# Query and key weights of a cross attention multiplied once at the start, the per-batch query product taken out, and part of a memory read issued as a transpose

## What is computed

```python
# end of the first block
out = Y * silu(gate) @ w_out.T
...
reads = jnp.moveaxis(reads, 0, 1).reshape(B, L, D)
out = out + ALPHA * (reads @ w_read.T)
return residual + out
...
# cross attention of Q (tokens) over K = V (context)
q = Q @ Wq + bq
k = K @ Wk + bk
v = V @ Wv + bv
scores = jnp.einsum('bqd,bkd->bqk', q, k) * scale
scores = jnp.where(pad_mask == 0, jnp.float32(-1000000000.0), scores)
w = jax.nn.softmax(scores, axis=-1)
out = jnp.einsum('bqk,bkd->bqd', w, v)
out = out @ Wo + bo
```

## Time and profile before

| what | value |
|---|---|
| median of three runs | 873.61 us |
| span of the profiled execution, first to last instruction | 869.8 us |
| PE busy | 830.7 us (96%) |
| ACT busy | 736.7 us (85%) |
| DVE busy | 725.3 us (83%) |
| POOL busy | 166.0 us (19%) |
| DMA, mean rate | 26 GB/s |

### The profile page before, as it was taken

One profiled execution on the slowest core, in us unless ns is written; L12 is line 12 of the kernel. 1 busy time (PEld: TensorE's weight loads), 2 busy tenths in 40 slices (PEclk: granted clock), 3 DMA queues, 4 the chain that ended last, 5 costly groups with the idle time before them and its releaser, 6 DMA issues.

```text
span 869.8 us, 21262 instructions
## 1 busy us (share of the span) xinstructions
PE 830.7 (96%) x7966; PEld 584.0 (67%) x7966; DVE 725.3 (83%) x2189; ACT 736.7 (85%) x1407; POOL 166.0 (19%) x198
## 2 busy tenths in 40 slices
PE   7899999999999999999999999999999999998874
PEld 4676767777767767777767767676767677654432
DVE  3653578989898999989898989999898988897775
ACT  3887789899898989899998989898998989784633
POOL 7101120312031131313120211312120310211110
PEclk9999999999999999999999999999999999998988
DMA  6100101010010101010100101001000000000000
GB/s 190 50 14 4 38 3 38 5 38 16 2 39 16 37 17 38 16 37 17 38 15 2 39 16 38 29 25 29 25 16 14 27 16 25 16 26 13 12 1 24
DMA packets 22403, 23.03 MB, mean 26 GB/s; under 512 B 11259, under 2 KB 13261, under 8 KB 22301
## 3 DMA queue, kind: packets, MB, share of 16 engines
q1 hardware_dynamic: 21868, 20.56, 7.8%
q10 hardware_dynamic: 432, 1.11, 0.4%
HBM read 16.68 MB, written 4.19 MB: 24 GB/s over the span
## 4 chain that ended last, share of the span: by engine, by line
PE 80%; ACT 7%; DVE 7%; issue 2%; DMA 1%; POOL 1%; SPq 1%; ACTq 0%; POOLq 0%; DVEq 0%
PE pM L2300 12%; PE pP L2252 8%; PE pP L2253 6%; PE pP L2254 6%; PE pDec L2287 3%; PE pY L2316 3%; PE pDec L2288 3%; PE pA L2379 3%; PE pA L2252 2%; PE pA L2351 2%; PE pC L2428 2%; PE pC L2388 2%; PE pA L2253 2%; PE pA L2254 2%; PE pD L2477 2%
## 5 line engine op out<-in xcount | busy, mean ns | idle before, releaser
L2252 PE MATMUL pP<-xn_hi,G_hi 128*128 128x256 f32 x512 | 163.0, 318 | 0.7 <-ACT P L737 0.7
L737 ACT ACTIVATE P<-pP 128x512 f32<-128x512 f32 x256 | 150.1, 599 | 7.8 <-PE pP L2254 6.6
L2253 PE MATMUL pP<-xn_lo,G_hi 128*128 128x256 f32 x512 | 143.8, 281 | 0.0
L2254 PE MATMUL pP<-xn_hi,G_lo 128*128 128x256 f32 x512 | 143.7, 281 | 0.0
L2300 PE MATMUL pM<-P,xnT 128*64 128x512 f32 x512 | 137.3, 614 | 1.9 <-DVE ML L1629 1.6
L599 POOL TENSOR_TENSOR rs_c<-ve_c,half_pow 128x4 f32<-128x4 f32 x48 | 49.1, 1023 | 405.0 <-DVE nm_c L1677 277.3
L2252 PEld LDWEIGHTS pP<-xn_hi,G_hi 128*128 128x128 f32 x512 | 96.5, 188 | 26.3 <-issue 13.9
L1629 DVE TENSOR_TENSOR ML<-pM,Lm 128x512 f32<-128x512 f32 x128 | 87.5, 684 | 22.1 <-PE pM L2300 19.2
L2253 PEld LDWEIGHTS pP<-xn_lo,G_hi 128*128 128x128 f32 x512 | 96.7, 189 | 2.9 <-issue 1.0
L2254 PEld LDWEIGHTS pP<-xn_hi,G_lo 128*128 128x128 f32 x512 | 96.5, 188 | 0.0
L746 ACT ACTIVATE Lm<-pDec 128x512 f32<-128x512 f32 x128 | 77.1, 602 | 21.3 <-PE pDec L2288 18.1
(11 more groups left out here) (242 smaller groups left out, 2026.1 us busy)
## 6 DMA issues: line engine op xcount, KB each, us to landing
x_in<-in_x SPq DMA_DIRECT2D x16, 256.0 KB, 3.3
cum_diag<-cum SPq DMA_DIRECT2D x256, 3.0 KB
x_res<-in_x SPq DMA_DIRECT2D x16, 256.0 KB, 2.6
ctxT<-in_ctx_t SPq DMA_DIRECT2D x16, 256.0 KB, 3.0
out_x<-r SPq DMA_DIRECT2D x16, 256.0 KB, 2.1
P<-in_wc ACTq DMA_DIRECT2D x2, 512.0 KB, 6.8
P<-in_wb SPq DMA_DIRECT2D x2, 512.0 KB, 8.6
fa<-in_w_t SPq DMA_DIRECT2D x1, 256.0 KB
```

The lines of the kernel that those rows point to most:

```text
L737: act.activation(P[:, half, 2 * pair:2 * pair + 2, 0:w], pP[k % 2][:, 0:2 * w].rearrange("p (h l) -> p h l", h=2), ACT.Copy).then_inc(p_co ...
L2252: pe.matmul(dst, w_hi, x_hi, start=True, stop=False)
L2253: pe.matmul(dst, w_hi, x_lo, start=False, stop=False)
L2254: return pe.matmul(dst, w_lo, x_hi, start=False, stop=True)
```

## The change

In the setup the kernel transposes Wq and Wk and multiplies them once, to `w_qk` = Wq Wk^T scaled. Per batch, `keys` uses `w_qk` in the place of Wk, and the scores are products of x1T itself with what `keys` gave. `queries` on PE and `copy_queries` on ACT go. The biases come back in three ways: Wq bk as a column that ACT adds in `copy_keys`; Wk bq as a half-wide product of `w_kb` with the context, issued once for each half of the partitions inside `attention_scores`; and the constant bq.bk as three more rows (32, 64 and 96) of the mask product, split in three bfloat16 parts. Since the context is now read until the scores, it gets two buffers. In `memory_read` the product with the identity becomes a transpose.

```diff
-C_K, C_VW, C_OUT, C_ST, C_VV, C_ACC, C_X1, C_Q, C_SC, C_EW, C_O = range(1, 12)
+C_K, C_VW, C_OUT, C_ST, C_VV, C_ACC, C_X1, C_SC, C_EW, C_O = range(1, 11)
...
-                    sp.wait_ge(c_mm.sem, c_mm.at(c - 1, C_VW))
-                    sp.dma_start(ctxT[:, 0:late_width(c)], ctx_t[row][:, cols]).then_inc(ctx_loaded.sem, 16)
+                    sp.wait_ge(c_mm.sem, c_mm.at(c - 2, C_SC))
+                    sp.dma_start(ctxT[c % 2][:, 0:late_width(c)], ctx_t[row][:, cols]).then_inc(ctx_loaded.sem, 16)
...
-            def copy_queries(c):
-                act.wait_ge(c_mm.sem, c_mm.at(c, C_Q))
-                act.activation(qT[:, 0:late_width(c)], pC[:, 0:late_width(c)], ACT.Identity, bias=bq_s[:, 0:1], scale=float(D) ** -0.5)\
-                   .then_inc(c_read.sem, 1)
...
             def weights():
-                step0(dve.tensor_copy(halves[:, :], halves_f[:, :]))
-                step0(dve.tensor_scalar(bq_s[:, :], bq_s[:, :], float(D) ** -0.5, None, ALU.mult))
+                step0(dve.memset(m_rows[:, :], 0.0))
+                step0(dve.memset(halves[:, :], 0.0))
...
+                step0(dve.tensor_scalar(bq_cols, ones, bq_s, None, ALU.mult))
+                step0(dve.tensor_scalar(bk_cols[:, 0:128], ones, bk_s, None, ALU.mult))
+                step0(dve.tensor_scalar(bk_cols[:, 128:256], ones, bk_s, None, ALU.mult))
...
+            def score_weights_copied():
+                dve.wait_ge(s_pe0, 2)
+                step0(dve.tensor_copy(r1[:, 0:2, :], tiles(pC[:, 0:256])))
...
+            def score_weights():
+                step0(dve.tensor_copy(halves[0:2, :], halves_f[:, :]))
+                for row in ROW_OF_PART:
+                    step0(dve.memset(halves[row:row + 1, :], 1.0))
+                dve.wait_ge(s_pe0, 3)
+                for dst, at in ((w_qk[:, :], slice(0, 128)), (qk_bias[:, :], slice(128, 129)), (w_kb[:, :], slice(192, 256)),
+                                (bias_left, slice(256, 512))):
+                    step0(dve.tensor_scalar(dst, pC[:, at], float(D) ** -0.5, None, ALU.mult))
+                for row in ROW_OF_PART:
+                    step0(dve.tensor_copy(bias_part, bias_left))
+                    step0(dve.tensor_copy(m_rows[row:row + 1, :], bias_part[row:row + 1, :]))
+                    step0(dve.tensor_tensor(bias_left, bias_left, bias_part, ALU.subtract))
...
                 decayed(0, 1)
+                score_weights_copied()
                 decayed(0, 2)
...
                 conv_taps(1, 1)
+                score_weights()
                 mask_values(0)
                 cum_high(1)
...
+            def score_weights_turned():
+                pe.wait_ge(s_dve0, DVE_COLUMNS)
+                pe.transpose(pC[:, 0:128], wq_s, id_f[:, :])
+                pe.transpose(pC[:, 128:256], wk_s, id_f[:, :]).then_inc(s_pe0, 1)
+
+            def score_weight_products():
+                pe.wait_ge(s_dve0, DVE_TURNED)
+                pe.matmul(pC[:, 0:128], wkT_s, wqT_s, start=True, stop=True)
+                pe.matmul(pC[:, 128:129], wqT_s, bk_s, start=True, stop=True)
+                pe.matmul(pC[:, 192:256], wkT_s, bq_cols[:, 0:L], start=True, stop=True)
+                pe.matmul(pC[:, 256:512], bq_cols, bk_cols, start=True, stop=True).then_inc(s_pe0, 1)
...
-                pe.matmul(pC[:, 0:w], wk_s[:, :], ctxT[:, 0:w], start=True, stop=True).then_inc(c_mm.sem, 1)
+                pe.matmul(pC[:, 0:w], w_qk[:, :], ctxT[c % 2][:, 0:w], start=True, stop=True).then_inc(c_mm.sem, 1)
...
-                    pe.matmul(bank(pC, t), out_tile(t), id_f[:, :], start=True, stop=False)
+                    pe.matmul(bank(pC, t), out_tile(t), id_f[:, :], start=True, stop=False, is_transpose=True)
                     last = pe.matmul(bank(pC, t), SM[:, t, :], vv[:, t, :], start=False, stop=True)
...
-            def queries(c):
-                c_turn(c, C_Q)
-                w = late_width(c)
-                pe.matmul(pC[:, 0:w], wq_s[:, :], x1T[:, 0:w], start=True, stop=True).then_inc(c_mm.sem, 1)
...
                 pe.matmul(pC[:, 0:nt * L], halves[:, :], m_rows[:, 0:nt * L], start=True, stop=False)
+                for part in range(2):
+                    pe.matmul(pC[64 * part:64 * part + 64, 0:nt * L], w_kb[:, :],
+                              tiles(ctxT[c % 2][:, 0:late_width(c)])[:, :, 64 * part:64 * part + 64], start=False, stop=False)
...
-                    last = pe.matmul(pC[64 * part:64 * part + 64, L * t:L * t + L], qT[:, L * s:L * s + L],
+                    last = pe.matmul(pC[64 * part:64 * part + 64, L * t:L * t + L], x1T[:, L * s:L * s + L],
                                      kT[:, L * s:L * s + L], start=False, stop=(t == nt - 1))
```

More of the change, by code:

```diff
@@ L49 @@
 PARTS = 3
+ROW_OF_PART = (32, 64, 96)
 DT_ROWS = 32 * (PARTS - 1) + H
@@ L202, in build @@
         mem = sb("mem", [128, 128])
-        wq_s = sb("wq_s", [128, 128])
-        wk_s = sb("wk_s", [128, 128])
+        w_qk = sb("w_qk", [128, 128])
+        w_kb = sb("w_kb", [128, L])
         wvo = sb("wvo", [128, 128])
-        bq_s = sb("bq_s", [128, 1])
-        bk_s = sb("bk_s", [128, 1])
+        qk_bias = sb("qk_bias", [128, 1])
         bo_b = sb("bo_b", [128, 128])
@@ L254, in build @@
         x_res = sb("x_res", [128, T, 128])
-        ctxT = sb("ctxT", [128, GT])
+        ctxT = [sb(f"ctxT{i}", [128, GT]) for i in range(2)]
         m_in = sb("m_in", [2, T, L], I32)
-        m_rows = sb("m_rows", [2, T * L], BF16)
+        m_rows = sb("m_rows", [ROW_OF_PART[-1] + 1, T * L], BF16)
         halves_f = sb("halves_f", [2, 128])
-        halves = sb("halves", [2, 128], BF16)
+        halves = sb("halves", [ROW_OF_PART[-1] + 1, 128], BF16)
         outT = sb("outT", [128, GT + 1])
@@ L399, in build @@
         w_write_s, w_read_s, wvt_s, wo_s = (u[:, 0, 128 * k:128 * k + 128] for k in range(4))
-        bv_s, decay_s = u[:, 1, 0:1], u[:, 1, 1:2]
+        bv_s, decay_s, bq_s, bk_s = (u[:, 1, k:k + 1] for k in range(4))
+        wq_s, wk_s = u[:, 1, 128:256], u[:, 1, 256:384]
+        wqT_s, wkT_s = r1[:, 0, :], r1[:, 1, :]
+        bq_cols, bk_cols = r1[:, 2, :], x2[0][:, 0:2, :].rearrange("p t d -> p (t d)")
+        bias_left = x2[0][:, 2:4, :].rearrange("p t d -> p (t d)")
+        bias_part = qi[:, 0, 0:T * L]
         wvg = fa[:, 1, :, :].rearrange("p a b -> p (a b)").rearrange("p (k d) -> p k d", d=128)
@@ L846, in copy_keys @@
                 act.wait_ge(c_mm.sem, c_mm.at(c, C_K))
-                act.activation(kT[:, 0:late_width(c)], pC[:, 0:late_width(c)], ACT.Identity, bias=bk_s[:, 0:1]).then_inc(c_read.sem, 1)
+                act.activation(kT[:, 0:late_width(c)], pC[:, 0:late_width(c)], ACT.Identity, bias=qk_bias[:, 0:1]).then_inc(c_read.sem, 1)
             def copy_context_values(c):
@@ L1573, in weights @@
                 step0(dve.tensor_scalar(flat(fcw[:, :, :]), flat(fcw[:, :, :]), ws[:, 0:1], None, ALU.mult))
+                step0(dve.tensor_scalar(bq_cols, ones, bq_s, None, ALU.mult))
+                step0(dve.tensor_scalar(bk_cols[:, 0:128], ones, bk_s, None, ALU.mult))
+                step0(dve.tensor_scalar(bk_cols[:, 128:256], ones, bk_s, None, ALU.mult))
+                assert done[0] == DVE_COLUMNS, done[0]
+            def score_weights_copied():
+                dve.wait_ge(s_pe0, 2)
+                step0(dve.tensor_copy(r1[:, 0:2, :], tiles(pC[:, 0:256])))
+                assert done[0] == DVE_TURNED, done[0]
+            def score_weights():
[10 more added lines that the diff above has]
+                    step0(dve.tensor_tensor(bias_left, bias_left, bias_part, ALU.subtract))
                 assert done[0] == DVE_SETUP, done[0]
@@ L2427, in context_values @@
                 for t in range(LATE[c]):
-                    last = pe.matmul(bank(pC, t), ctxT[:, 128 * t:128 * t + 128], wvo[:, :],
+                    last = pe.matmul(bank(pC, t), ctxT[c % 2][:, 128 * t:128 * t + 128], wvo[:, :],
                                      start=True, stop=True)
@@ L2539, in fill @@
                 head_pair(0, 1, 2)
+                score_weights_turned()
                 head_pair(0, 1, 3)
@@ L2544, in fill @@
                 head_pair(0, 1, 4)
+                score_weight_products()
                 scores(0, 2)
@@ L2622, in fill @@
                 head_pair(2, 0, 3)
-                queries(0)
                 project(2, A_GATE[1], 3)
@@ L2685, in fill @@
                 project(3, A_GATE[0], 2)
-                queries(1)
                 head_values(2, 2)
@@ L2827, in drain @@
                 head_pair(12, 0, 3)
-                queries(10)
                 head_values(11, 1)
@@ L2896, in drain @@
                 project(13, A_GATE[0], 2)
-                queries(11)
                 head_pair(13, 0, 3)
@@ L3034, in drain @@
                 project(15, A_GATE[0], 2)
-                queries(13)
                 decay(14, 5)
@@ L3094, in drain @@
                 x1_transposed(14)
-                queries(14)
                 head_values(15, 3)
```

(1 more changed line is left out.)

19 lines of the change are left out of this document (4 added, 15 removed).

## The result

In 15 runs of each kernel, taken beside each other, the changed one took 875.08 us at the median (873.11 to 876.49) and the kernel before 872.45 (870.87 to 873.88). The ratio is 1.0028, with a 95% interval of 1.0021 to 1.0036: slower by 2.4 us. The profiled execution spans 871.9 us, 2.1 more than the one of before.

The account below looks back on a forecast made before the run. The prediction took the period as bound by ACT's list up to head pair 4 and PE's list behind it. Loop -4.8 and setup +6.9 gave +2.1 on 873.61, 875.7, rounded to 876.0 us; range 865.5 to 881.0.

Parts of the forecast that it names:

- The period is a stretch that ACT fills and one that PE fills: Body loop, 48.07 us: ACT's list fills 20.61 up to head pair 4, PE's list the other 27.46.
- First stretch -0.58: Body, ahead of head pair 4: the query copy leaves ACT's list, 0.58 us less per period.
- The sign that was named: Body: PE arrives nearly 1 us early somewhere before head pair 4 and waits for ACT's P.
- Bias +0.43: Between mask and scores on PE: two half-wide products add 0.43 us per period, bounds 0.43 and 0.86.
- rival C: In the scores: the bias halves run one behind the other, +0.43 more in 14 batches, 881.7 us; chance 0.12.
- Other batches: Outside the eight body batches: batches 0, 1 and 10 to 13 give -2.4 us, 14 and 15 give -1.2.
- Setup on PE +1.2: Setup: two transposes and products of 128, 1, 64 and 256 columns add 1.2 us on PE.
- Block 4.9: Setup on DVE: 17 steps ahead of the mask and cum_high(1) take 4.9 us, bounds 3.7 and 5.9.
- Wait 4.0: Setup: PE waits 4.0 us for cum_rest at the gate projection, bounds 1.5 and 5.0.
- Clock +1.7: Behind the setup wait: a lower granted clock on PE loses 1.7 us, bounds 0 and 3.4.
- Rival B: Loop: all of PE's savings count, 14 batches at -1.01 us, 865.2 us in total; chance 0.24.
- rival D: Setup: DVE's block is hidden and only PE's 1.2 us is left, 870.0 us in total; chance 0.08.

Follow-up runs that it names:

- the cut: Changed kernel with the 17 setup steps on DVE split: eight ahead of group 1's second convolution half, nine behind group 2's row statistics; 868.37 us.
- ACT's spare copy: Changed kernel with a spare 128x512 activation on ACT where the query copy stood; 881.52 us, ratio 1.0107.
- PE's spare product: Changed kernel with a spare 512-column float32 product on PE where the query product stood; 880.71 us, ratio 1.0096.
- the transposes: Changed kernel with the memory read's four transposes turned back to products with the identity; 875.40 us, ratio 1.0028.
- ACT's order: Changed kernel with DVE's setup block split in two, and ACT copying P of pair 2 ahead of the feed-forward activation; 866.54 us, ratio 0.9936.
- the same turn in ACT's order: Kernel before, with ACT copying P of pair 2 ahead of the feed-forward activation and the query copy; 872.15 us, ratio 0.9992.
- a second bias pair: Changed kernel with the two half-wide bias products issued twice; 881.12 us, ratio 1.0107.
- warm products: Changed kernel with 18 spare bfloat16 products of 512 columns on PE ahead of the waiting gate projection in the setup; 873.12 us, ratio 1.0001.

## Why the prediction was right

The forecast was 876.0 (872.45 + 2.1 by the runs of before that stand beside it would be 874.6), and 875.08 was measured. The profiled span came out at the forecast 871.9. But two terms were off by 1.2 us each, in opposite directions: the setup cost 8.1 where +6.9 was forecast, and the loop gave 6.0 where 4.8 was forecast. That the two errors cancelled is luck. The 8.1 and 6.0 are of one pair of profiles; the medians make it 8.0 (6.5 and the 1.5 left by the cut) and 5.6.

- *The period is a stretch that ACT fills and one that PE fills.* Shown for the first: ACT's spare copy costs its whole length, PE's spare product half of it, the transposes nothing, and ACT's order alone moves head pair 4. All that is the changed kernel. In the kernel before, PE's own list came to head pair 4 only some 0.03 us ahead of ACT's copy, and the same turn in ACT's order gave nothing that can be told: the stretch was as much PE's as ACT's, which the full 20.55 of 20.61 couldn't show. The forecast of this term holds all the same, for PE lost more than ACT did and then waited. For the second it is shown only in part: a second bias pair counts in full, the first doesn't, because DVE's ML was due nearly as late. DVE was busy for 25.69 of 27.46 there, and its order at this one place was not in the sum.
- *First stretch -0.58:* -0.59. The sign that was named, PE nearly 1 us early and waiting for P, shows as a wait of 0.20 there and as the 0.48 that the spare product filled.
- *Bias +0.43:* the second pair took 0.43 and mask to next products of P grew by 0.44, so the row of L2300 was the right one to take, and the two halves run at once (rival C falls). The second stretch grew by only 0.29, for head pair 4 to mask took 0.10 less and what lies behind the scores 0.04 less. So a period lost 0.30, twice the forecast 0.15, and eight batches gave 2.4.
- *Other batches:* batches 0, 1 and 10 to 13 gave 3.0 (forecast 2.4), the last two 0.6 (1.2).
- *Setup on PE +1.2:* +1.4. *Block 4.9:* 5.34, as from start to start a step took 0.03 to 0.09 more than its own time (62.27 to 62.56 for one of 0.20); its upper bound of 5.9 is 6.1 by the prices given for it. *Wait 4.0:* 4.30. *Clock +1.7:* 2.4. All three were sized low, by 0.2, 0.3 and 0.7; the clock was the weakest, taken from a window of a mean that another stall had made. PE's +1.4 is of one pair of profiles, and in that of the kernel before with ACT's order, the same program so far, the same copy of P came 2.16 late, so this term isn't shown to 0.2.
- *Rival B (PE's account)* falls by the period, 47.77 and not 47.1, and by the spare copy and the spare product; *rival D (hidden block)* by the wait of 4.30.

That part of PE's new wait ahead of head pair 4 could be had by ACT's order was not in the prediction; it follows from its reading of the loop. Head pair 4 came 0.22 earlier, and it was worth 0.25 per period.

## What to carry to other kernels

Where the busiest engine shows no idle time, cut one period at the place where it starts right behind another engine's result, and count a saving only in the stretch that its own engine sets; then move that other engine's result ahead, or the saving isn't seen. Find out as well when the busiest engine's own list would have reached that place: here the two were level to 0.03 us, and DVE, a third, was close behind. One-time work has no fixed price: 17 small steps cost 6.5 us ahead of a value that PE was about to need and next to nothing in the waits nearby. A wait of PE like these two, of 3.3 and 4.3 us, is to be priced with the clock behind it; in the one of 4.3, spare products gave that part back.

## What the runs showed of the hardware

The time behind a wait was lost at the lower clock twice: 2.4 us behind 4.30, and some 1.7 (by the mean clock) to 2.1 (5.4 less 3.32) behind 3.32. PE's timeline behind the last head pair ahead of the scores, before and after:

```profile
442.37 0.28 PE L2254 MATMUL pP<-xn_hi,G_lo 128*128 128x256 f32 x1
442.58 0.28 PE L2446 MATMUL pC<-m_rows,halves 2*128 2x256 bf16 x1
```

```profile
447.29 0.28 PE L2281 MATMUL pP<-xn_hi,G_lo 128*128 128x256 f32 x1
447.40 0.28 PE L2468 MATMUL pC<-m_rows,halves 97*128 97x256 bf16 x1
```

The mask product with 97 rows starts 0.11 us behind the product ahead of it (447.29 and 447.40); the one with 2 rows started 0.21 behind (442.37 and 442.58 in the trace of before). That is the 0.10 that head pair 4 to mask became shorter; no wait on another engine is seen there in either, and why it is so stays open. Single profiled executions differ by up to 3.3 us in the first 58 us: ACT's copy of P at 58.57 came 1.40 late in the changed kernel and 4.66 late in the one with warm products, whose program is the same that far. So small differences were read from periods and from several runs, not from one span.
